# Two-layer transformer block: the keys of the second layer's head attention fetched for two steps at once

## The reference

```python
# layer 0, over the sequence
scores = einsum('blhd,bmhd->bhlm', q * scale, k)      # 1024 x 1024 for each of 16 heads
o = einsum('bhlm,bmhd->blhd', softmax(scores), v)
# layer 1, over the heads of one token
attn = einsum('nthd,ntkd->nthk', q * scale, k)        # 16 x 16 for each of 2048 tokens
out = einsum('nthk,ntkd->nthd', softmax(attn), v)
out = out.transpose(0, 2, 1, 3).reshape(n, t, d)
# both
x = x + gate_msa * proj(attention(modulate(layernorm(x))))
x = x + gate_mlp * fc2(gelu(fc1(modulate(layernorm(x)))))
```

## Time and profile before

| | us |
|---|---|
| median of 3 runs | 952.34 |
| lowest, highest | 948.98, 955.22 |
| the profiled execution | 951.97 |
| its span, first to last instruction | 950.2 |

### The profile page before, as it was taken

One profiled execution on the slowest core, in us unless ns is written; L12 is line 12 of the kernel. 1 busy time (PEld: TensorE's weight loads), 2 busy tenths in 40 slices (PEclk: granted clock), 3 DMA queues, 4 the chain that ended last, 5 costly groups with the idle time before them and its releaser, 6 DMA issues. The chain is left out here.

```text
span 950.2 us, 16650 instructions
## 1 busy us (share of the span) xinstructions
PE 809.5 (85%) x6096; PEld 369.0 (39%) x6096; DVE 648.8 (68%) x1273; ACT 531.9 (56%) x751; POOL 264.6 (28%) x327
## 2 busy tenths in 40 slices
PE   1588999999999999998887979998778885899996
PEld 0252222222222222222234546555445553565564
DVE  2848788888888888888338654562488878845521
ACT  3450577777676777777874724661457624446630
POOL 2311011214453411010016236222133446411122
PEclk9996699999999999999998999999799996999998
DMA  9110000111112010000400020103564630000000
GB/s 264 41 51 19 20 27 26 26 45 30 32 34 62 31 35 16 22 15 8 102 2 10 2 75 2 37 1 98 136 149 120 154 79 2 32 1 26 25 26 26
DMA packets 51999, 45.35 MB, mean 48 GB/s; under 512 B 23770, under 2 KB 41108, under 8 KB 51927
## 3 DMA queue, kind: packets, MB, share of 16 engines
q1 hardware_dynamic: 47391, 35.98, 14.8%
q10 hardware_dynamic: 4536, 8.41, 2.8%
HBM read 27.66 MB, written 9.46 MB: 39 GB/s over the span
## 5 line engine op out<-in xcount | busy, mean ns | idle before, releaser
L870 DVE TENSOR_REDUCE row_max<-ps 128x1 f32<-128x512 f32 x512 | 322.3, 683 | 64.2 <-PE ps L1589 63.1
L1355 ACT ACTIVATE probs<-ps 128x1024 f32<-128x1024 f32 x256 | 248.4, 1018 | 52.8 <-PE ps L1616 52.0
L1589 PE MATMUL ps<-stack_area 54*128 54x512 f16 x512 | 162.0, 400 | 25.6 <-DVE row_max L870 20.5
L1628 PE MATMUL ps<-probs,mlp_area 128*32 128x512 f32 x1024 | 137.1, 608 | 0.4 <-ACT probs L1355 0.4
L1616 PE MATMUL ps<-stack_area 56*128 56x512 f16 x512 | 110.1, 384 | 9.6 <-ACT probs L1355 9.3
L1701 PE MATMUL ps<-mlp_area,w_fc 128*128 128x512 f16 x504 | 111.7, 382 | 7.2 <-DVE v_sb L862 4.9
L1589 PEld LDWEIGHTS ps<-stack_area 54*128 54x128 f16 x512 | 39.0, 94 | 201.6 <-DVE row_max L870 187.9
L1718 PE MATMUL ps<-w_fc,mlp_area 128*128 128x288 f16 x864 | 110.7, 291 | 4.0 <-DVE mlp_area L1006 4.0
L1394 ACT ACTIVATE mlp_area<-ps 128x512 f32<-128x512 f32 x72 | 43.0, 597 | 102.2 <-PE ps L1701 100.9
L1718 PEld LDWEIGHTS ps<-w_fc,mlp_area 128*128 128x128 f16 x864 | 85.2, 99 | 28.7 <-DVE mlp_area L1006 3.5
L1014 DVE SCALAR_TENSOR_TENSOR probs<-ps,fc_bias 128x288 f32<-128x288 f32 x32 | 14.6, 457 | 101.9 <-PE ps L1718 101.9
(11 more groups left out here) (157 smaller groups left out, 1077.0 us busy)
## 6 DMA issues: line engine op xcount, KB each, us to landing
qkv_rows<-part_area ACTq DMA_DIRECT2D x24, 252.0 KB
stack_area<-tokens SPq DMA_DIRECT2D x128, 36.0 KB
x_sb<-in_x SPq DMA_DIRECT2D x4, 576.0 KB, 7.6
stack_area<-part_area SPq DMA_DIRECT2D x64, 36.0 KB
w_raw<-in_L_cond_W_fc SPq DMA_DIRECT2D x4, 576.0 KB
tokens<-qkv_rows SPq DMA_DIRECT2D x64, 36.0 KB
v_sb<-qkv_rows SPq DMA_DIRECT2D x16, 144.0 KB
w_raw<-in_L_cond_fc_w SPq DMA_DIRECT2D x4, 576.0 KB
```

The lines of the kernel that those rows point to most:

```text
L870: nc.vector.reduce_max(row_max[:, p % 2, t, j, half:half + 1], bank(bk), AX.X).then_inc(max_done, 1)
L1355: nc.scalar.activation(probs[:, n % 2, 2 * c:2 * c + 2, :].rearrange("p h n -> p (h n)"), ps[:, 2 + 2 * c:4 + 2 * c, :].rearrange("p b n - ...
L1589: nc.tensor.matmul(bank(bk), stacks[rows, p % RING, 0, t * P:(t + 1) * P], stacks[rows, p % RING, 1, half * 512:(half + 1) * 512], start=T ...
L1628: mm = nc.tensor.matmul(bank(6)[at:at + VW, :], v_pad[:, TB * (p // BPAIR) + n, 2 * (p % BPAIR) + j, :], probs[:, n % 2, 2 * c + j, :], st ...
```

## The change

Keys are fetched for two steps with one `fetch_k(u)`: 4 DMAs with runs of 64 numbers (256 bytes) into one of two buffers, each twice as large. Half as many key DMAs are issued, 32 in place of 64. The key rows are ordered by pairs of steps. `k_ring` and the queries behind it fill `tokens` to its end, so the odd `v_cells` move into the area of the fc2 weights, and job 8, whose weights would be written there, moves from step 17 to tile 10, job 9 from tile 11 to tile 12. SP's order changes: queries of pieces 2 and 3 are fetched at steps 4 and 8 in place of 5 and 9, and the keys that open a piece (steps 8 and 9, 12 and 13) right behind them. POOL's memset covers all of `tokens`.

```diff
-        HC, NPIECE, NSTEP, MT, KBUF = 32, 4, 16, 7, 3
+        HC, NPIECE, NSTEP, MT, KBUF, KSTEPS = 32, 4, 16, 7, 2, 2
...
-        k_ring = tokens[:, 0:6144].rearrange("p (r a k c) -> p r a k c", r=KBUF, a=4, k=H)
-        q_rows = [f.rearrange("p (h c) -> p h c", h=H) for f in (tokens[:, 6144:8192], free4[:, 0:2048])]
+        k_ring = tokens[:, 0:8192].rearrange("p (r a k c) -> p r a k c", r=KBUF, a=4, k=H)
+        q_rows = [f.rearrange("p (h c) -> p h c", h=H) for f in (tokens[:, 8192:10240], free4[:, 0:2048])]
...
-        v_cells = [f.rearrange("p (c d) -> p c d", d=HC) for f in (free_v[:, 2048:4096], tokens[:, 8192:10240])]
+        fc2_area = w_fc2[:].rearrange("p s f n -> p (s f n)").bitcast(F32)
+        v_cells = [f.rearrange("p (c d) -> p c d", d=HC) for f in (free_v[:, 2048:4096], fc2_area[:, 0:2048])]
...
-        JOB_STEPS = {2: 5, 7: 6, 12: 7, 17: 8}
+        JOB_STEPS = {2: 5, 7: 6, 12: 7}
...
-        JOB_TILES = {11: 9, 14: 10}
+        JOB_TILES = {10: 8, 12: 9, 14: 10}
...
-                return (cols.rearrange("p (x s n) -> p s x n", x=8, s=4), "p (s x n) -> p s x n", dict(s=4, x=8))
+                return (cols.rearrange("p (x s n) -> p s x n", x=8, s=2), "p (s x n) -> p s x n", dict(s=2, x=8))
...
-            def fetch_k(k):
-                if k >= KBUF:
-                    sp.wait_ge(cell_mm, k - KBUF + 1)
-                i, j = divmod(k, 4)
-                src = qkv_rows[i, C:2 * C, :].rearrange("(k d) (j a c) -> a j d k c", d=D, a=4, j=4)
+            def fetch_k(u):
+                if u >= KBUF:
+                    sp.wait_ge(cell_mm, KSTEPS * (u - KBUF + 1))
+                i, j = divmod(u, 2)
+                src = qkv_rows[i, C:2 * C, :].rearrange("(k d) (j a c) -> a j d k c", d=D, a=4, j=2)
...
             fetch_k(0)
-            fetch_k(1)
             stored(MT)
             sp.wait_ge(pads_set, 1)
             fetch_v(0)
-            fetch_k(2)
+            fetch_k(1)
...
-                if k % 4 == (0 if i == 1 else 1) and i < NPIECE:
+                if k % 4 == 0 and i < NPIECE:
                     stored(MT * i + 3)
                     fetch_q(i)
-                if k + KBUF < NSTEP:
-                    if k % 4 == 1:
-                        stored(MT * i + 5)
-                    fetch_k(k + KBUF)
+                u = k // KSTEPS + KBUF
+                if k % KSTEPS == 0 and KSTEPS * u < NSTEP:
+                    if u % 2 == 0:
+                        stored(MT * (u // 2) + 5)
+                    fetch_k(u)
                 if k % 4 == (2 if i == 1 else 3) and i < NPIECE:
                     stored(MT * (i + 1))
                     fetch_v(i)
...
-                    nc.gpsimd.memset(tokens[:, 0:8192], 0.0).then_inc(zeros_set, 1)
+                    nc.gpsimd.memset(tokens[:], 0.0).then_inc(zeros_set, 1)
...
-                pe.wait_ge(k_in[k % KBUF], 64 * (k // KBUF + 1))
+                u, half = divmod(k, KSTEPS)
+                if half == 0:
+                    pe.wait_ge(k_in[u % KBUF], 64 * (u // KBUF + 1))
...
-                keys = k_ring[:, k % KBUF].rearrange("p a k (t n) -> p (a k) t n", t=2)
+                keys = k_ring[:, u % KBUF].rearrange("p a k (t n) -> p (a k) t n", t=2)
...
-                                              keys[:, :, :, at],
+                                              keys[:, :, :, 16 * half + at],
```

4 lines of the change are left out of this document (2 added, 2 removed).

## The result

| | before | after |
|---|---|---|
| median of 4 runs each, us | 952.94 | 967.67 |
| lowest, highest | 948.98, 955.22 | 965.19, 973.20 |
| ratio after / before, with 95% interval | | 1.0167 (1.0111 to 1.0223) |
| the profiled execution, its span | 951.97, 950.2 | 973.20, 971.4 |

The change makes the kernel slower by 1.7% in this measurement. The forecast was 961.0 in a range of 954.5 to 966: the sign of the sum was right, its size too small, and the time lies outside the range. Two more measurements of the same kernel, taken with the experiments, gave 1.0119 (1.0085 to 1.0153) and 1.0131 (1.0090 to 1.0172), medians of 965.42 and 965.76 beside 953.7. The change costs some 12 to 15 us.

A forecast was written before the change was run, and what follows sets the result against it. DVE's waits were taken to bound the head attention and PE the last MLP. Terms 2.2 + 1.1 - 0.5 + 6.6 = +9.4 us on the profiled 951.97 gave 961.4, rounded down to 961.0, range 954.5 to 966.

The forecast's parts named there:

- part 3: Step 8: job 6's load, now issued behind piece 2's opening keys, lands late and ACT waits for it; +2.2 us.
- part 4: Values of piece 3 are issued sooner, with one key DMA group less ahead of them; -0.5 us (-1.0 to 0).
- part 5: Behind the head attention: jobs 8, 9 and 10 share w_raw, a serial chain that starts the last MLP later; +6.6 us.
- What bounds the kernel: DVE's waits count in the head attention, PE carries the last MLP; a delay ahead of the MLP reaches the end in full.
- Which waits matter: Waits for keys at steps 8 and 12 and for values cost DVE at most 7.5 us; step 3's wait costs nothing.
- The price of a run: Key fetches: a run of 256 bytes costs one DMA engine 22 ns, between 13 and 26.
- Part 2: Opening keys of pieces 2 and 3 reach steps 8 and 12 later, and DVE idles for both; +1.1 us each.
- Part 6: The rest: POOL's longer memset, the doubled stride of score matmuls and the saved DMA issues cost or gain 0.
- the rival that everything adds up higher: Dearer runs, later job 6 load, stride cost and low clock through tile 15: +11.6 us, 964, at most +13.7; chance 0.28.
- The one that isn't slower: Keys, not stores, set the openings of pieces 2 and 3, so 7.5 us go against the tail's 6.6: 951; chance 0.05.
- the one with the hidden tail: Other work behind the same end hides the tail's delay: +2.8 us, 955; chance 0.05.
- the rival in which only the tail counts: Head attention +1.0 for cheap runs and an earlier job 6 load, values -1.0, tail 6.0: +5 us, 957; chance 0.14.

The follow-up runs named there:

- experiment 5: Kernel before with job 6's load alone moved behind the opening keys of piece 2, runs of 128 bytes: 956.28 us, ratio 1.0023.
- experiment 10: As experiment 9 but runs of 128 bytes, 8 DMAs a pair: 960.31 us (1.0055) with one wait per pair, 958.02 (1.0046) with a semaphore per step.
- experiment 1: Kernel before with only the new places of jobs 8 and 9, behind the head attention: 961.07 us, ratio 1.0086.
- experiment 9: Changed kernel with job 6's load early, piece 1's values ahead of the second pair of keys, own raw buffers for jobs 9 and 10: 956.30 us, 1.0035.
- experiment 2: Changed kernel with raw buffers of their own for jobs 9 and 10, in the free key ring: 961.02 us, ratio 1.0087.

## Why the prediction was wrong, point by point

The steps that failed are, in this order, part 3 (job 6's load priced at +2.2, where DVE lost 2.4 to 4.4 us to it), part 4 (a term for the values of piece 1 left out, where DVE waited 0.5 to 1.6 us) and part 5 (+6.6 for the tail, where it lost 7.7).

- *What bounds the kernel* held: a delay ahead of the MLP came through, and step 3's wait went without a gain. *Which waits matter* held for step 12 alone. I read DVE's 2.57 us at step 8 as a wait for keys, though its bracket names ACT. Keys up to 7.5 us after their issue left it at 2.6 us, so the 7.5 us that I said could be had from keys and values were 2.6 too many.
- *The price of a run*: 19 ns measured, 22 taken.
- *Part 2, keys of steps 8 and 12, +1.1 each* (in the sum only step 12's, since part 3's larger term stood at step 8). Issue to scores was 6.6, 4.6 and 6.0 us at step 8 in the three executions of after, and 6.1, 5.8 and 5.9 at step 12; in the kernels with keys as before it was 4.0 to 4.95 and 4.3 to 5.25. By the means this is +1.1 and +1.3. DVE's idle time behind step 12 was 3.9 to 5.4 in the six traces with before's fetches, and 5.5 to 6.3 in after's three. The size was nearly right, but "at both DVE idles for them" was wrong: at step 8 it doesn't. The base was lucky: before's profiled execution had ACT's table load at 686.3 us, the others of its kind at 687.8 to 690.2, and from there on it took as long as they.
- *Part 3, job 6's load, +2.2.* This step failed first, in its size: the path (load, ACT's high part, widening, output, DVE) was the right one. I had the load issued 1.7 us behind the keys' first issue and landed 6.8 behind it. It was issued 2.2 to 2.5 behind and used at 7.3 to 8.8, in after's three executions ACT waited 2.4, 4.2 and 4.4 us, and DVE idled that much longer. In experiment 5, with keys as before, ACT waited 3.5. From issue to use I gave the load 5.1 us (729.9 to 735), and it took 6.4, 5.2 and 6.5.
- *Part 4, values.* Here a term was missing. I looked at the values of piece 3, which come sooner (no wait is left there), and not at those of piece 1, which SP now issues behind both pairs of keys. DVE waited for them in all six traces with this order, 0.46 to 2.55 us (0.46 to 1.56 in after's three). The head attention lost 3.7 us counted from S and 5.4 from ACT's table load, where the forecast's terms for it gave +2.8.
- *Part 5, the tail, +6.6.* The mechanism was right in each row: the serial loads, PE idle for 7 us, the low clock. It measured +7.7 (7.8 with the tables alone). Of my two cases (+6.3 with the clock back for tile 15, +7.4 without) I took a value near the lower; tile 15 ran at the low level too, and the chain ahead of tile 14 was 0.4 us longer.
- *Part 6* nearly held: the memset found its cover, and the score group with the doubled stride takes 2.06 us in place of 1.95. It takes 1.95 again in experiment 10, where the numbers lie 64 bytes apart as before, so the stride is what costs these 0.1 us, and "both pay alike" was not quite so.
- *The rounding down.* From 961.4 I went to 961.0 for slack that I didn't see. None showed; the unseen terms were costs.
- *The rivals.* The 11.4 to 13.1 us by the traces are the rival that everything adds up higher (+11.6, 964, at most +13.7): its low clock through tile 15 and its later load came, its 26 ns didn't, and of its 0.9 us a group for the stride 0.1 did. The one that isn't slower and the one with the hidden tail are excluded by the waits above, and experiment 1 shows the tail's loss by itself. The sum of the rival in which only the tail counts was off: 1.0 - 1.0 + 6.0 is +6, 958, and not +5, 957, and the lower end of part 5 was +6.3.
- *The range.* Its top of 966 left no room for the spread between measurements: of the three medians of the changed kernel two lie within it, and the one that the forecast was for does not.

What stays open: how the load and the values share the loss of the head attention (alone neither edit gained anything, the load in ten runs and the values in four; both early gained 2.9 us in six, with intervals of some 3 us each way), why ACT stands earlier against PE in some executions than in others, why the first median of after was 2 us above the two later ones, and why the same idle time of PE is followed by a low clock in one kernel and not in another.

## What to carry to other kernels

Where an edit reorders one queue by hand, write down every transfer that is now issued later, and for each who waits for it next; here one such wait was priced too low and one was missed, while the transfers that the change was about were priced well. Read in the bracket who ended an idle time before you give it to a wait that stands near it: DVE's at step 8 was ACT's, not the keys'. A buffer that holds load, high part and low part of a job is a chain: moving one more job into the stretch behind the last cover costs a whole load, and the idle time of TensorE that it makes costs again by the clock. Two delays on one path can each be worth nothing when taken out alone (here both together gave some 3 us), so take out both before you call either harmless. Fix the baseline of a sum from more than one execution if you can, and compare traces by stretches from one common row to the next, not by their ends; try rows of more than one engine.

## What was not expected of the hardware

- Executions of one program differ by 4 us at S, with the clock that PE is granted (0.83 against 0.91 in the same 20 us), and executions whose last MLP is the same program by 1.7 us in it (0.88 against 1.00 in 14 us near its end).
- Behind 3.7 us of idle time the next twelve matmuls took 0.91 and 0.90 us for six in one kernel (experiment 9, granted 1.00) and 1.62 and 1.64 in another (10, granted 0.50); in experiment 2 the first six took 0.91 and the next six 1.65.
- A load of 576 KB took 4.0 us from issue to use on an empty queue and 5.0 to 6.5 behind 4 key DMAs and ahead of 4 more or 8.
- Score matmuls that read numbers 128 bytes apart took 2.06 us for a group of 32, with 64 bytes between them 1.95.
